# Squares of a step-size series moved from ScalarE to GpSimd, quantised outputs taken earlier, and the seams of a state scan put in another order

## The reference

```
# layer 1, feed-forward, on h = layernorm(x)
absmax = max(|h|) over the last axis;  scale = max(absmax, 1e-7) / 127
q = clip(round(h / scale), -128, 127)
x = x + tanh(g_ffn[1]) * float16((q @ weight.T) * scale * w_scale + bias)
# layer 2, SSM, on the context and z = layernorm(x)
u     = silu(conv(in_proj @ ctx) + conv_b)
x_dbl = x_proj @ u                        # 16 rows dt, 16 rows B, 16 rows C
delta = softplus(dt_proj @ dt + dt_b)     # the step sizes
state = state * exp(delta * A) + (delta * u) * B        # over 512 positions, 16 states
y     = sum over the 16 states of state * C;  y = y + D * u;  y = y * silu(z)
x = x + tanh(g_xattn[2]) * y
```

## Time and profile before

| | us |
|---|---|
| median of 3 runs (3408.71 to 3416.11) | 3413.54 |
| profiled execution | 3416.8 |
| its span | 3415.1 |
| the series' block | about 1056 to 1286 |
| the scan's block | about 1287 to 1800 |
| DVE busy over the whole span | 2322.0 (68%) |
| POOL busy over the whole span | 1131.4 (33%) |

### The profile page before, as it was taken

How to read it: one execution, slowest core, us unless ns; L and a number is a source line. 1 busy time by engine, 2 the same in 40 slices (tenths; PEclk the granted TensorE clock), 3 DMA queues, 4 the chain that set the end, 5 groups by cost and what they waited for, 6 DMA issues and landing times. The chain is left out here.

```text
span 3415.1 us, 42603 instructions
## 1 busy us (share of the span) xinstructions
PE 2536.0 (74%) x14172; PEld 1217.5 (36%) x14172; DVE 2322.0 (68%) x3741; ACT 1604.3 (47%) x2262; POOL 1131.4 (33%) x815
## 2 busy tenths in 40 slices
PE   2987897799679735766673899809788888668990
PEld 1532333344234311222222677605322222324660
DVE  6665763465857788899886566565688885555664
ACT  2544553244232665455541556505466675224870
POOL 5755763020001115666660222055510000002434
PEclk9988999799779857898895899959799999779995
DMA  3650321111000000000001777545502201104995
GB/s 130 199 174 13 93 63 75 46 38 37 0 4 11 1 0 1 0 0 0 0 0 52 256 248 234 166 121 199 187 11 75 63 14 63 50 25 146 317 306 166
DMA packets 162831, 305.94 MB, mean 90 GB/s; under 512 B 33299, under 2 KB 80671, under 8 KB 160246
## 3 DMA queue, kind: packets, MB, share of 16 engines
q1 hardware_dynamic: 139462, 223.49, 18.9%
q0 software_dynamic: 23216, 80.49, 8.3%
HBM read 210.34 MB, written 93.32 MB: 89 GB/s over the span
## 5 line engine op out<-in xcount | busy, mean ns | idle before, releaser
L2100 DVE TENSOR_REDUCE ac_nmax<-ac_M 128x1 f32<-128x512 f32 (+1 forms) x768 | 497.2, 687 | 152.0 <-PE ac_M L1914 147.2
L2078 ACT ACTIVATE ac_PT<-ac_S 128x1024 f32<-128x1024 f32 x384 | 371.2, 1018 | 160.0 <-PE ac_S L1949 137.1
L2924 POOL TENSOR_TENSOR sc_hc<-sc_h,sc_cs 128x1024 f32<-128x1024 f32 x128 | 300.6, 2354 | 170.3 <-DVE sc_h L3038 113.1
L3038 DVE TENSOR_TENSOR_SCAN sc_h<-sc_dA,sc_dB 128x1024 f32<-128x1024 f32 x128 | 292.1, 2283 | 7.0 <-ACT sc_dA L3004 7.0
L2959 PE MATMUL sc_y<-sc_hc,ident 128*128 128x512 f32 x512 | 254.1, 626 | 2.3 <-POOL sc_hc L2924 2.3
L3004 ACT ACTIVATE sc_dA<-ss_delta,sc_A 128x511 f32<-128x511 f32 x256 | 166.0, 682 | 30.8 <-DVE sc_h L3038 30.3
L3030 DVE TENSOR_TENSOR sc_dB<-ss_du,sc_b 128x1024 f32<-128x1024 f32 x128 | 156.2, 1220 | 27.8 <-PE sc_b L2937 17.2
L2937 PE MATMUL sc_b<-ss_bc,sc_sel 128*128 128x512 f16 x128 | 54.7, 428 | 159.9 <-DVE sc_dB L3030 126.6
L3009 ACT ACTIVATE sc_cs<-sc_c 128x512 f32<-128x512 f32 x128 | 76.2, 596 | 203.2 <-POOL sc_hc L2924 160.3
L1914 PE MATMUL ac_M<-KT,QT 64*128 64x512 f16 (+1 forms) x384 | 141.5, 431 | 39.8 <-DVE ac_nmax L2100 23.0
L1001 DVE SCALAR_TENSOR_TENSOR mo_up16l<-mo_up,mo_up16h 128x1408 f16<-128x1408 f32 (+1 forms) x80 | 117.1, 1465 | 72.0 <-ACT mo_up16h L945 71.8
(11 more groups left out here) (495 smaller groups left out, 6195.8 us busy)
## 6 DMA issues: line engine op xcount, KB each, us to landing
slot_results<-mo_o SPq DMA_DIRECT2D x56, 512.0 KB
mo_up<-in_w_gate SPq DMA_DIRECT2D x24, 704.0 KB, 5.6
mo_up<-in_w_up SPq DMA_DIRECT2D x24, 704.0 KB, 7.0
keys_t<-ap_kto SPq DMA_DIRECT2D x32, 512.0 KB, 2.7
queries_t<-ap_qto SPq DMA_DIRECT2D x32, 512.0 KB, 2.7
mo_up<-in_exp_up SPq DMA_DIRECT2D x32, 512.0 KB
mo_dn<-in_exp_down SPq DMA_DIRECT2D x32, 512.0 KB
mo_dn<-in_w_down SPq DMA_DIRECT2D x24, 512.0 KB
```

The lines of the kernel that those rows point to most:

```text
L2078: nc.scalar.activation(PT[:, n % PTB, :, :], psS[:, 2 * (n % 2):2 * (n % 2) + 2, :], ACT.Exp, scale=SCALE / (SQK * SQK)).then_inc(exp_done, 1)
L2100: last = v.tensor_reduce(out[:, :, 0], sc[:, 0:MAIN], AX.X, ALU.max)
L2924: nc.gpsimd.tensor_tensor(hc[:, m % RC, :, :], h[:, m % RH, :, :], cs[:, m % 2, :].unsqueeze(1).to_broadcast([P, W, S]), ALU.mult).then_in ...
L3038: nc.vector.tensor_tensor_scan(h[:, m % RH, :, :].rearrange("p c s -> p (c s)"), dA[:, m % 2, :, :].rearrange("p c s -> p (c s)"), dB[:, m ...
```

## The change

Five edits.

1. The squares move from ACT to POOL as an elementwise product. They lose the factor 0.5, which the four constants of the series take up. POOL's list becomes square, bias, product for each half.
2. One reduction of absolute values stands for the minimum, the maximum and the small instruction that joined them.
3. The outputs are taken two tiles behind in place of three, from tile 10 on: `quantised(10)` holds two outputs, and `quantised(11)` two residuals. The rest of the tail moves with it.
4. In the scan `rows(m+6)` and `rows(m+7)` stand behind the first and second `summed` of a group and no longer in front of the first, and `collect` and `gate` come one unit earlier (n == 1).
5. `gates(b)` comes at n == 2 of a batch's first group (n == 6 for the first batch), and no longer at n == 8.

```diff
@@ layer_ffn1 @@
-        squares_at = {8: (0,), 10: (1,), 12: (2,), 14: (3,)}
...
             for t in range(7):
                 biases(t)
+            square(0)
+            biases(7)
+            biases(8)
             inputs(0)
...
+            for i in range(1, 6):
+                square(i)
+                biases(i + 8)
+                inputs(i)
+            square(6)
             inputs(6)
             biases(14)
+            square(7)
             biases(15)
             inputs(7)
...
+            def square(i):
+                pool.wait_ge(s_done, i + 1)
+                nc.gpsimd.tensor_tensor(t2[:], half(t1, i % 2), half(t1, i % 2), ALU.mult).then_inc(q_done, 1)
...
-            def square(i):
-                act.wait_ge(s_done, i + 1)
-                nc.scalar.activation(t2[:], half(t1, i % 2), ACT.Square, scale=0.5).then_inc(q_done, 1)
...
-                if t >= 3:
+                if 3 <= t <= 10:
                     output(t - 3)
-                nc.vector.tensor_reduce(l, y[:, v, :], AX.X, ALU.min)
-                c.link(nc.vector.tensor_reduce(i, y[:, v, :], AX.X, ALU.max))
-                c.link(nc.vector.scalar_tensor_tensor(out=i, in0=l, scalar=-1.0, in1=i, op0=ALU.mult, op1=ALU.max))
+                if t >= 10:
+                    output(t - 2)
+                c.link(nc.vector.tensor_reduce(i, y[:, v, :], AX.X, ALU.max, apply_absolute_value=True))
...
-                if t >= 4:
+                if 4 <= t <= 10:
                     residual(t - 4)
+                if t == 11:
+                    residual(7)
+                if t >= 11:
+                    residual(t - 3)
...
             ratio(6)
-            output(13)
-            residual(12)
-            softplus(6)
-            ratio(7)
-            output(14)
             residual(13)
-            softplus(7)
-            output(15)
             for t in (11, 12, 13):
                 statistics(t)
+            softplus(6)
+            output(14)
+            ratio(7)
+            output(15)
             residual(14)
+            statistics(14)
+            softplus(7)
             residual(15)
@@ ssm_scan_block @@
-                if gp and n == 2:
+                if gp and n == 1:
                     gate(gp - 1)
...
                     if gp:
                         turned(gp - 1)
                     rows(m + LAG + 1)
-                    rows(m + LAG + 2)
-                elif n > 2:
+                elif n < 3:
+                    rows(m + LAG + 1)
+                elif n > 3:
                     rows(m + LAG)
                 summed(m)
...
-                if p == 0 and n == NS // 2:
+                if p == 0 and n == (2 if gp else 6):
...
-                if gp and n == 2:
+                if gp and n == 1:
                     collect(gp - 1)
```

More of the change, by code:

```diff
@@ L2516, in layer_ffn1 @@
         qT = sb("qT", [P, 2, KD, P], F16)
-        sc, inv, least = sb("sc", [P, 4]), sb("inv", [P, 2]), sb("least", [P, 2])
+        sc, inv = sb("sc", [P, 4]), sb("inv", [P, 2])
         o32, o16 = sb("o32", [P, 2, D]), sb("o16", [P, 2, D], F16)
@@ L2576, in inputs @@
                 nc.gpsimd.tensor_tensor(half(du, i), half(delta, i), half(u, i), ALU.mult).then_inc(du_done, 1)
-            for t in range(8):
+            def square(i):
+                pool.wait_ge(s_done, i + 1)
+                nc.gpsimd.tensor_tensor(t2[:], half(t1, i % 2), half(t1, i % 2), ALU.mult).then_inc(q_done, 1)
+            for t in range(7):
                 biases(t)
+            square(0)
+            biases(7)
+            biases(8)
             inputs(0)
[L2580 to L2590, removed]
+            for i in range(1, 6):
[3 more added lines that the diff above has]
+            square(6)
             inputs(6)
             biases(14)
+            square(7)
             biases(15)
@@ L2731, in _ @@
                     projected(m // KD - 1)
-                for i in squares_at.get(m, ()):
-                    square(i)
                 if m >= KD and m % KD >= 2:
@@ L2736, in _ @@
             projected(B - 1)
-            square(4)
             inverse(6)
             evacuate(14)
-            square(5)
             inverse(7)
             evacuate(15)
-            for i in range(4):
+            for i in range(2 * B):
                 skips(i)
[L2745 to L2750, removed]
         @block.vector
@@ L2777, in quantised @@
                 v = t % 2
-                r, i, l = sc[:, t % 4:t % 4 + 1], inv[:, v:v + 1], least[:, v:v + 1]
+                r, i = sc[:, t % 4:t % 4 + 1], inv[:, v:v + 1]
                 c.link(nc.vector.tensor_scalar(y[:, v, :], env.x[:, t, :], agg[:, t, 0:1], rstd[:, t:t + 1],
                                                ALU.subtract, ALU.mult))
-                if t >= 3:
+                if 3 <= t <= 10:
                     output(t - 3)
-                nc.vector.tensor_reduce(l, y[:, v, :], AX.X, ALU.min)
-                c.link(nc.vector.tensor_reduce(i, y[:, v, :], AX.X, ALU.max))
-                c.link(nc.vector.scalar_tensor_tensor(out=i, in0=l, scalar=-1.0, in1=i, op0=ALU.mult, op1=ALU.max))
+                if t >= 10:
+                    output(t - 2)
+                c.link(nc.vector.tensor_reduce(i, y[:, v, :], AX.X, ALU.max, apply_absolute_value=True))
                 if t >= 4:
@@ L2817, in softplus @@
                 dve.wait_ge(q_done, i + 1)
-                c.link(nc.vector.tensor_scalar(z, t2[:], c4, None, ALU.mult))
-                for cc in (c3, c2, c1):
+                c.link(nc.vector.tensor_scalar(z, t2[:], c4 / 256, None, ALU.mult))
+                for cc in (c3 / 64, c2 / 16, c1 / 4):
                     c.link(nc.vector.scalar_tensor_tensor(out=z, in0=z, scalar=cc, in1=t2[:], op0=ALU.add, op1=ALU.mult))
@@ L2835, in _ @@
             ratio(6)
-            output(13)
-            residual(12)
-            softplus(6)
-            ratio(7)
-            output(14)
             residual(13)
-            softplus(7)
-            output(15)
             for t in (11, 12, 13):
                 statistics(t)
+            softplus(6)
+            output(14)
+            ratio(7)
+            output(15)
             residual(14)
+            statistics(14)
+            softplus(7)
             residual(15)
-            statistics(14)
             statistics(15)
```

## The result

The changed kernel takes 3382.8 us (3380.2 to 3388.0, 4 runs) against 3411.1 before: ratio 0.9919, 95% interval 0.9899 to 0.9939. It is 28.4 us faster. The forecast was 20 us and 3393.5, from a median before of 3413.5 that one more run has made 3411.1.

What follows compares the result with a forecast made beforehand. DVE was taken to bound both blocks. Series 26.1 + 4.3 - 8.5 - 4.4 - 4.5 - 3.3 = 9.7 and scan 32.1 - 22.1 = 10.0 saved gave -20: 3393.5 us, range 3383 to 3405.

Steps and rivals of the forecast that it cites:

- squares behind ACT's list: Series' block: DVE's waits for ACT's square go, except the first, which moves to `bc_low`; 14.8 us saved.
- `inverse` behind a late product: Series' block: the later two of three 10.6 us waits for ACT's `inverse` go; some 7.1 us saved.
- one reduction less, tiles 11 to 15: Series' block: one reduction and L2785, 0.68 + 0.16 a tile, leave DVE; 4.2 us saved, possibly 0.8.
- stalls beside GpSimd, net: Series' block: DVE held beside POOL costs 8.5 in tiles, 4.4 at `ratio`, 4.5 in the tail; 4.3 us of stalls go.
- the gates: Scan's block: ACT's decay is late by 4.9 us at seams 2, 4, 6 (14.7), 1.8 in first batch; 7.0 removed.
- PE's clock, 3.5: Scan's block: after a seam PE is granted 1.2 GHz and sums slowly; 0.5 us a seam, 3.5 in all.
- `rows` -16.5: Scan's block: b rows issued between the sums are no longer late; 16.5 us of DVE's waits removed.
- `update` -8.6: Scan's block: `update` no longer waits for the turned y, except behind the last group; 8.6 us removed.
- squares give back: Rival, series' block: POOL's instructions hold DVE in full, block 3 us slower, scan saves its 10; 3405 us, chance 0.16.
- doesn't do what it says at the seams: Rival, scan's block: gates' wait at three seams and slower sums eat all 10 us; 3404 us, chance 0.08.
- stays at 1.2 GHz: Rival, scan's block: PE stays slow behind each seam, 0.8 us lost a unit; time up to 3427 us, chance 0.04.
- Ports and clock cost less: Rival, both blocks: L2790 and L2793 pass POOL, no clock loss; 17 + 13.5 = 30 saved, 3383 us, chance 0.12.

Runs made afterwards that it cites:

- e7: Changed kernel with minimum, maximum and their small combination again in place of one reduction of absolute values, in all 16 tiles: 3386.0 us, ratio 0.9916.
- e11: Kernel before with only collect and GpSimd's gate of y one state earlier, rows and gates as before: 3408.9 us, ratio 0.9995.
- e12: Changed kernel with update ahead of the fourth state's scan, gates at the ninth state for every batch, and an earlier tile's statistics ahead of L2774: 3375.4 us.
- e13: As e12, but with the gates at the third state of a batch, as in the changed kernel: 3377.7 us, ratio 0.9897.
- e8: Changed kernel with each of the eight squares made twice on GpSimd, the second behind the first: 3398.0 us, ratio 0.9954.
- e4: Changed kernel with update one DVE instruction earlier, ahead of the scan of the fourth state: 3379.8 us, ratio 0.9898.
- e10: Kernel before with only the rows behind a seam moved, one after each sum of the new group: 3403.7 us, ratio 0.9979.

## Why the prediction was right, step by step

The waits that the forecast wanted gone are gone, and the stalls that it wanted to pay for them came. One size was well off, and in the scan's block one cost had the wrong cause. Series' block, forecast and measured (marks, and their counterparts; "measured" is behind `bc_low(1)`, at 1142.45):

| step | forecast | measured |
|---|---|---|
| squares behind ACT's list | -14.8 | -14.7 |
| `inverse` behind a late product | -7.1 | -7.4 |
| one reduction less, tiles 11 to 15 | -4.2 | -4.0 (e7: -3.5) |
| stalls beside GpSimd, net | +13.1 | +6.5 |
| ACT last at the end | +3.3 | +3.1 |
| `bc_low(1)` | 0 | +1.1 |

The forecast's sum is -9.7. The measured rows, with -0.7 for one `output` that moved ahead of the mark, give -16.1 against -15.7 by the block's length. The +1.1 at `bc_low(1)` need be no cost of the change: with the list of before the mark came 85.0 us after the block's start in one execution and 86.0 in another (e11), and with the one list of e12 and e13 86.1 and 84.7. But the changed kernel and most of those made from it have the longer time, so whether the change has a share in it stays open.

**The term that was mis-sized is the stalls** (8.5 in the tiles, 4.4 for `ratio`, 4.5 in the tail, less 4.3 that go: +13.1). By groups behind the mark:

```profile
L2800 DVE SCALAR_TENSOR_TENSOR f_t<-ss_du,f_t 128x1024 f32<-128x1024 f32 x7 | 19.9, 2841 | 0.4
L2801 DVE SCALAR_TENSOR_TENSOR f_t<-f_t 128x1024 f32<-128x1024 f32 x7 | 9.5, 1360 | 0.2
L2755 DVE SCALAR_TENSOR_TENSOR x_res<-f_o,tanh_gates,x_res 128x512 f32<-128x512 f16 x9 | 7.8, 878 | 0.0
L2776 DVE TENSOR_SCALAR f_y<-f_y,f_inv 128x512 f32<-128x512 f32 x5 | 6.3, 1267 | 0.2
L2808 DVE TENSOR_SCALAR ss_du<-f_t 128x1024 f32<-128x1024 f32 x7 | 5.6, 799 | 0.0
```

Against the sums of before in the same stretch (17.3, 8.6, 8.4, 2.4, 5.9) that is +2.6, +0.9, -0.6, +3.9 and -0.3. In the tiles I had the square at 2.34. It took 2.13 and began 0.4 us before I had it, and both come off a stall that is a small difference of two times (1.0 a tile, not 1.8, and 0.5 in tile 11, not 1.3). Beyond the tiles, the tail's stalls came smaller (0.9, 1.2 and 0.3 for 1.3, 1.9 and 1.3) and its wait for a square not at all. That the square as it stands is covered, and that more of GpSimd's time than the cover holds is paid by DVE for more than half, is shown by e8 (five more squares of some 2 us in the tiles, 8.5 us of holding).

L2776 and, where GpSimd reaches it, L2779's counterpart are held (e8); the reduction and the statistics never are (0.68 and 0.69 throughout). So the trace agrees with the rule of the Trainium skill that the prediction weighed ("SBUF — State Buffer", section "Who interferes with whom").

Scan's block: the -10.4 of the loop came out as forecast, -10, but **two wrong terms cancelled**, the gates (4.3 us too dear) and the late b row (3.3 too cheap). That the sum is so near is luck.

- The gates were forecast to cost 14.7 + 1.8 - 7.0 = 9.5 more than before; their wait went from 7.0 to 12.2, so 5.2. What failed is "two table loads and four activations": the first load, 1.28 us, does not wait for the gate. (The forecast's own figures, 13.1 less 8.3 to 8.4, give 4.7 to 4.8 a seam and not the 4.9 that it took; measured 3.50.)
- "PE's clock, 3.5" is the step that named half of a cause. The b row was 6.8 us late in seven seams, because the first sum waits for `update`'s reads and then runs slowly. The wait stands in lines that the diff leaves alone, and I overlooked it; e4 took the 6.8 away and left the clock at 0.50.
- `rows` -16.5 and `update` -8.6 held (13.1 to 3.7, behind the last group alone), and `collect` 1.5 for 2.1. e10 and e11 show that these two belong together.

Of the rivals, "squares give back" is excluded by the series' block (-15.7, where it had +3), "doesn't do what it says at the seams" by the loop's -10.4, and "stays at 1.2 GHz" by the unit of the scan, which still takes 3.5 us between seams (1396.11 to 1399.64). "Ports and clock cost less" had 3383, which is what was measured, but that is luck: in it L2776 passes GpSimd and the clock costs nothing, and the trace has L2776 held for 1.0 us in four tiles and the slow sum at every seam. Its parts, -17 and -13.5, don't come out either; the blocks gave -15.7 and -10.4, and the medians 2.3 us more than these two, inside their noise.

Left open: 1.2 us of the scan's waits (they sum to -11.6, the loop to -10.4), 0.9 of the 2.2 in e4, why the stretch in front of `bc_low(1)` takes now 84.8 and now 86.1 us, and what the b row would do if the sum ran at full clock.

## What to carry to other kernels

Where two engines hold each other up by turns, don't add durations: write both engines' instructions on one clock, and put the ones that need one input or none (reductions, statistics) under the other engine's instruction; a stall is the small difference of two sums, so 0.4 us off in a start halves it. When a wait is removed, list every semaphore that the next instruction in line still waits for, also those in lines that the change doesn't touch: here that was a PSUM tile not yet read. Together with a slow sum it cost 6.8 us, and moving one instruction got them back. Two edits that cure the same late engine aren't worth their sum (9.0 and 11.4 gave 15.7), and two that share a seam may be worth more (8.4 and 3.8 gave 16.5).

## What the runs showed of the hardware that I had not expected

- A DVE instruction on one element a partition with two SBUF inputs is held like a large one: 0.98 us against 0.16 (e7).
- GpSimd's product of a tile with itself took 1.89 us (128x1024, f32) in the changed kernel's last square and in seven of e8's eight second ones, and that of two tiles 2.34 to 2.36 in most cases. The squares of 2.13 us began each while DVE ran L2765; that the 0.24 are a wait for it is argued, not shown.
```profile
1255.39 1.89 POOL L2578 TENSOR_TENSOR f_t<-f_t 128x1024 f32<-128x1024 f32 x1 [2.42 <-DVE f_t L2802]
```
- DVE gets in between two GpSimd instructions that follow back to back, if it is already waiting, and the later one then takes 1.44 us for 1.26 (e8).
- ACT's table load for an activation runs ahead of that activation's wait on a semaphore (1401.60, against 1405.89 for the activation itself).
